# Attention loop of a fused perceiver layer: ScalarE spreads the turned output, GpSimd scales it by its reciprocals and adds the residual one batch later

## The reference, cut to what matters

```python
# x (16, 64, 1024); ctx (16, 1601, 256); mask (64, 1601)
q = layernorm(x).reshape(b, s, 8, 4, 32)                 # 8 kv heads, 4 query heads each
k = v = ctx.reshape(b, 1601, 8, 32)
scores = einsum('bsgrd,btgd->bgrst', q, k) / sqrt(32) + mask
out = einsum('bgrst,btgd->bsgrd', softmax(scores), v)
x = x + out.reshape(b, s, 1024)                          # this stage, the one that is changed
x = x + gated_ffn_with_top_k_zeroing(layernorm(x))       # untouched
x = x + mixture_of_8_low_rank_experts(layernorm(x))      # untouched
```

## Time and profile before

| | |
|---|---|
| median of 3 runs | 1584.75 us (1582.42 to 1586.70) |
| profiled execution, its own time | 1583.21 us |
| its span in the trace | 1580.8 us |
| attention loop, first to last mask addition | 45 to 645 us |
| PE, DVE, ACT, POOL busy, whole span | 1402, 1066, 664, 849 us |

### The profile page before, as it was taken

One profiled execution on the slowest core, in us unless ns is written; L12 is line 12 of the kernel. 1 busy time (PEld: TensorE's weight loads), 2 busy tenths in 40 slices (PEclk: granted clock), 3 DMA queues, 4 the chain that ended last, 5 costly groups with the idle time before them and its releaser, 6 DMA issues.

```text
span 1580.8 us, 30023 instructions
## 1 busy us (share of the span) xinstructions
PE 1402.1 (89%) x12775; PEld 1033.1 (65%) x12775; DVE 1065.7 (67%) x1424; ACT 664.1 (42%) x777; POOL 848.9 (54%) x410
## 2 busy tenths in 40 slices
PE   3899999999998999489999999999897788899975
PEld 3554555455554555289999998878776667687852
DVE  7788888888888888580000008998819888855663
ACT  2777777777777777312111116152410320011211
POOL 0577777777777777522233222333335565587840
PEclk9999999999999999789999999999999998899997
DMA  7032322232222230312322245565537855765612
GB/s 283 2 101 83 110 100 100 98 109 101 99 85 98 85 111 2 149 43 72 116 100 72 101 144 192 178 227 199 195 118 279 293 179 173 279 191 176 178 66 81
DMA packets 111466, 212.18 MB, mean 134 GB/s; under 512 B 8208, under 2 KB 84064, under 8 KB 107232
## 3 DMA queue, kind: packets, MB, share of 16 engines
q1 hardware_dynamic: 90224, 187.67, 34.6%
q10 hardware_dynamic: 21104, 22.55, 4.7%
HBM read 167.99 MB, written 42.21 MB: 133 GB/s over the span
## 4 chain that ended last, share of the span: by engine, by line
PE 42%; DVE 7%; DMA 4%; issue 3%; POOL 1%; ACT 1%; SPq 0%; DVEq 0%; ACTq 0%; POOLq 0%
PE ffn_bank L1794 15%; PE ffn_bank L1817 13%; PE ffn_bank L1848 11%; DMA ffn_u_raw<-w_up_t 2%; DVE ffn_h_lo L1497 1%; PE ffn_bank L1910 1%; PE ffn_bank L1875 1%; PE ffn_bank L1831 1%; DVE ffn_ln_stats L98 1%; DMA ffn_sx<-s 1%; DVE ffn_below L1393 1%; DMA sk<-ffn_sx 1%; DMA ffn_xt<-x 1%; POOL ffn_u_lo L1339 0%; DVE ffn_db L1408 0%
## 5 line engine op out<-in xcount | busy, mean ns | idle before, releaser
L761 POOL TENSOR_TENSOR fast_pair<-fast_probs 128x1024 f32<-128x1024 f32 x192 | 462.9, 2411 | 184.5 <-ACT fast_probs L879 107.4
L817 DVE TENSOR_TENSOR fast_masked<-fast_scores,fast_mask_t 128x1024 f32<-128x1024 f32 (+1 forms) x416 | 490.0, 1219 | 72.4 <-PE fast_scores L937 66.1
L879 ACT ACTIVATE fast_probs<-fast_masked 128x1024 f32<-128x1024 f32 (+1 forms) x416 | 440.0, 1058 | 145.4 <-DVE fast_masked L817 131.0
L937 PE MATMUL fast_scores<-fast_qT,fast_kraw 32*128 32x256 f32 (+1 forms) x3328 | 242.7, 406 | 46.7 <-DVE fast_masked L817 45.9
L937 PEld LDWEIGHTS fast_scores<-fast_qT,fast_kraw 32*128 32x128 f32 (+1 forms) x3328 | 150.4, 183 | 135.0 <-DVE fast_masked L817 94.7
L954 PE MATMUL fast_o_acc<-fast_probs,fast_vraw 128*32 128x256 f32 (+1 forms) x3328 | 228.4, 389 | 1.7 <-ACT fast_probs L879 1.7
L1794 PE MATMUL ffn_bank<-ffn_g_hi,ffn_z_hi 128*128 128x344 f32 x512 | 165.9, 324 | 2.6 <-ACT ffn_res L1658 2.6
L1382 DVE TENSOR_SCALAR ffn_cut<-ffn_total 128x2 f32<-128x2 f32 x4 | 0.7, 166 | 246.7 <-ACT ffn_mag L1662 246.7
L1351 POOL TENSOR_TENSOR ffn_d_lo<-ffn_d_raw,ffn_d_hi 128x1024 fp32r<-128x1024 f32 x66 | 163.2, 2472 | 5.3
L1794 PE MATMUL ffn_bank<-ffn_g_lo,ffn_z_hi 128*128 128x344 f32 x512 | 164.8, 322 | 0.0
L1794 PE MATMUL ffn_bank<-ffn_g_hi,ffn_z_lo 128*128 128x344 f32 x512 | 164.6, 322 | 0.0
(11 more groups left out here) (147 smaller groups left out, 1924.9 us busy)
## 6 DMA issues: line engine op xcount, KB each, us to landing
ffn_d_raw<-w_down SPq DMA_DIRECT2D x63, 512.0 KB, 3.7
fast_kraw<-ctx_t SPq DMA_DIRECT2D x32, 800.5 KB, 5.8
fast_vraw<-ctx_nat SPq DMA_DIRECT2D x16, 1536.0 KB
ffn_g_raw<-w_gate SPq DMA_DIRECT2D x8, 1376.0 KB
s<-ffn_res SPq DMA_DIRECT2D x8, 1376.0 KB, 6.1
ffn_mag<-s SPq DMA_DIRECT2D x8, 1376.0 KB, 9.8
ffn_sx<-s SPq DMA_DIRECT2D x8, 1376.0 KB, 6.9
sk<-ffn_sx SPq DMA_DIRECT2D x8, 1376.0 KB, 6.3
```

The lines of the kernel that those rows point to most:

```text
L761: pool.tensor_tensor(pair[:, n % PAIRS], both[:, :, 0, :], both[:, :, 1, :], ALU.add).then_inc(paired, 1)
L817: dve.tensor_tensor(into, of, m, ALU.add).then_inc(mask_added, 1)
L879: act.activation(probs[0:r, g % RING, hp * HALF:(hp + 1) * HALF], masked[0:r, h % SLOTS, :], ACT.Exp).then_inc(exp_done, 1)
L937: last = pe.matmul(scores[0:r, (2 * g + h // 2) % SLOTS, h % 2, i * 256:(i + 1) * 256], kraw[q, b % BUFS, u, c * P:c * P + r], qT[q, b, u, ...
```

## The change

ScalarE gets a new step, `spread_output` (L910 on in the changed file, its copies are L919), at the step of the turn, behind that step's exponentials. It copies the turned numerators from PSUM to `xo` in final order, two copies of 64x256, unscaled. VectorE's `normalise` keeps only two reciprocals of 64x8, written in the order of the heads, and now waits for both `o_turned` and `o_spread`; what it signals is `rden_ready`, for which TensorE's `weigh` waits in place of `o_normed`. Once a tile GpSimd multiplies all 128x1024 of `xo` by the reciprocals, broadcast over 32 elements each (`scale_output`, L764), in the `LAST` step after the tile's last normalisation, and adds `xres` (`add_residual`, L768) in the `LAST` step of the next batch. `xo` has two buffers. The store of a tile stands one batch later in SyncE's queue. For the last tile, the multiplication and the addition follow directly after the last reciprocals.

```diff
+        SPREAD1_AT = 17
+        SPREAD0_AT = 10
+        SCALE_AT = PER + 19
+        ADD_AT = SCALE_AT + PER
...
-                if b >= 3 and b % 2 == 1:
-                    sp.wait_ge(x_added, b // 2)
+                if b >= 4 and b % 2 == 0:
+                    sp.wait_ge(x_added, b // 2 - 1)
...
+            def scale_output(t):
+                pool.wait_ge(o_spread, 4 * t + 4)
+                pool.wait_ge(rden_ready, 4 * t + 4)
+                rows_of = xo[:, t % 2, :].rearrange("p (m d) -> p m d", d=HD)
+                by = rden[:, t].rearrange("p u g q h -> p (u g q h)").unsqueeze(2).broadcast_to([P, NH, HD])
+                pool.tensor_tensor(rows_of, rows_of, by, ALU.mult).then_inc(o_normed, 1)
+
+            def add_residual(t):
+                pool.wait_ge(o_normed, t + 1)
+                pool.tensor_tensor(xres[:, t, :], xo[:, t % 2, :], xres[:, t, :], ALU.add).then_inc(x_added, 1)
...
+            for g in range(GROUPS + 7):
+                if g < GROUPS:
+                    add_pair(g)
+                if g >= SCALE_AT and (g - SCALE_AT) % (2 * PER) == 0:
+                    scale_output((g - SCALE_AT) // (2 * PER))
+                if g >= ADD_AT and (g - ADD_AT) % (2 * PER) == 0:
+                    add_residual((g - ADD_AT) // (2 * PER))
+            add_residual(TILES - 1)
...
                 dve.wait_ge(o_turned, n + 1)
-                dve.reciprocal(rden[:, n], turned[:, 1, :, :, 0]).then_inc(rden_ready, 1)
-                dve.wait_ge(rden_ready, n + 1)
-                out = xo[b2 * S:(b2 + 1) * S, :].rearrange("s (u g q h d) -> s u h q g d", u=2, g=HALF_G, q=2, h=2)
+                dve.wait_ge(o_spread, n + 1)
+                out = rden[b2 * S:(b2 + 1) * S, t].rearrange("s u g q h -> s u h q g")
                 for h in range(2):
-                    half = slice(h * S, (h + 1) * S)
-                    last = dve.tensor_tensor(out[:, u, h], turned[half, 0],
-                                             rden[half, n].unsqueeze(3).broadcast_to([S, 2, HALF_G, HD]), ALU.mult)
-                last.then_inc(o_normed, 1)
-                if b2 == 1 and u == 1:
-                    dve.wait_ge(o_normed, n + 1)
-                    dve.tensor_tensor(xres[:, t, :], xo[:, :], xres[:, t, :], ALU.add).then_inc(x_added, 1)
+                    last = dve.reciprocal(out[:, u, h], turned[h * S:(h + 1) * S, :, :, 0])
+                last.then_inc(rden_ready, 1)
...
+            def spread_output(n):
+                b, u = divmod(n, 2)
+                t, b2 = divmod(b, 2)
+                act.wait_ge(o_turned, n + 1)
+                if b2 == 0 and u == 0 and t >= 2:
+                    act.wait_ge(x_added, t - 1)
+                out = xo[b2 * S:(b2 + 1) * S, t % 2, :].rearrange("s (u g q h d) -> s u h q g d", u=2, g=HALF_G, q=2, h=2)
+                for h in range(2):
+                    turned = o_acc[h * S:(h + 1) * S, u, 0:256].rearrange("p (q g d) -> p q g d", q=2, g=HALF_G)
+                    last = act.copy(out[:, u, h], turned)
+                last.then_inc(o_spread, 1)
...
-                        pe.wait_ge(o_normed, 2 * (b - 1) + u + 1)
+                        pe.wait_ge(rden_ready, 2 * (b - 1) + u + 1)
```

More of the change, by code:

```diff
@@ L661, in attention_fast @@
         od_sb = sb("od_sb", [P, 512], F32)
-        rden = sb("rden", [P, UNITS, 2, HALF_G], F32)
-        inside = sb("inside", [P, UNITS * 2 * HALF_G], F32)
+        rden = sb("rden", [P, TILES, 2, HALF_G, 2, 2], F32)
+        inside = sb("inside", [P, TILES * NH], F32)
         row_inside = sb("row_inside", [S, 1], F32)
-        xo = sb("xo", [P, D], F32)
+        xo = sb("xo", [P, 2, D], F32)
         eye = sb("eye", [P, P], F32)
@@ L692, in attention_fast @@
         rden_ready = sem("rden_ready")
+        o_spread = sem("o_spread")
         o_normed = sem("o_normed")
@@ L741, in _ @@
                     load_v(sp, b + BUFS)
-                if b >= 3 and b % 2 == 1:
-                    sp.wait_ge(x_added, b // 2)
-                    sp.dma_start(x1[(b // 2 - 1) * P:(b // 2) * P, :], xres[:, b // 2 - 1, :]).then_inc(x1_stored, 16)
-            sp.wait_ge(x_added, TILES)
-            sp.dma_start(x1[(TILES - 1) * P:TILES * P, :], xres[:, TILES - 1, :]).then_inc(x1_stored, 16)
+                if b >= 4 and b % 2 == 0:
+                    sp.wait_ge(x_added, b // 2 - 1)
+                    sp.dma_start(x1[(b // 2 - 2) * P:(b // 2 - 1) * P, :], xres[:, b // 2 - 2, :]).then_inc(x1_stored, 16)
+            for t in range(TILES - 2, TILES):
+                sp.wait_ge(x_added, t + 1)
+                sp.dma_start(x1[t * P:(t + 1) * P, :], xres[:, t, :]).then_inc(x1_stored, 16)
             sp.wait_ge(x1_stored, 16 * TILES)
@@ L752, in _, with add_pair @@
             pool.memset(ones[:, :], 1.0).then_inc(ones_ready, 1)
-            for g in range(GROUPS):
+            def scale_output(t):
[7 more added lines that the diff above has]
+                pool.tensor_tensor(xres[:, t, :], xo[:, t % 2, :], xres[:, t, :], ALU.add).then_inc(x_added, 1)
+            def add_pair(g):
                 if g % PER == LAST:
-                    continue
+                    return
                 n = pairs_before(g)
@@ L822, in normalise @@
                 t, b2 = divmod(b, 2)
[L823 removed]
+                turned = o_acc[:, u, 256:512].rearrange("p (q g d) -> p q g d", q=2, g=HALF_G)
                 dve.wait_ge(o_turned, n + 1)
[L825 to L827 removed]
+                dve.wait_ge(o_spread, n + 1)
+                out = rden[b2 * S:(b2 + 1) * S, t].rearrange("s u g q h -> s u h q g")
                 for h in range(2):
[L829 to L835 removed]
+                    last = dve.reciprocal(out[:, u, h], turned[h * S:(h + 1) * S, :, :, 0])
+                last.then_inc(rden_ready, 1)
             for g in range(GROUPS + 8):
@@ L843, in _ @@
                         normalise(2 * ((g - at) // PER) + u)
-            every = rden[:, :, :, :].rearrange("p n q g -> p (n q g)")
+            dve.wait_ge(rden_ready, UNITS)
+            every = rden[:, :, :, :, :, :].rearrange("p t u g q h -> p (t u g q h)")
             dve.tensor_scalar(inside[:, :], every, RDEN_LEAST, None, ALU.is_ge).then_inc(checked, 1)
@@ L888, in _ @@
             act.wait_ge(mask_turned, 1)
-            for g in range(GROUPS + 4):
+            def spread_output(n):
[9 more added lines that the diff above has]
+                last.then_inc(o_spread, 1)
+            for g in range(GROUPS + 6):
                 if g < GROUPS:
@@ L895, in _ @@
                         copy_output(2 * ((g - at) // PER) + u)
+                for u, at in ((0, SPREAD0_AT), (1, SPREAD1_AT)):
+                    if g >= at and (g - at) % PER == 0 and (g - at) // PER < B:
+                        spread_output(2 * ((g - at) // PER) + u)
         @block.tensor
```

1 line of the change is left out of this document (removed).

## The result

The changed kernel took 1543.66 us (median of 4 runs, 1540.49 to 1551.21) against 1583.59 of the kernel before beside it (4 runs, 1581.32 to 1586.70). The ratio is 0.9753, 95% interval 0.9713 to 0.9794. Repeated on other chips it took 1546.94 and 1549.67 us (5 runs each; ratios 0.9775, interval 0.9747 to 0.9804, and 0.9776, interval 0.9756 to 0.9796). The median of all 14 runs is 1546.7.

The account below looks back on a forecast made before the run. The ring between TensorE's scores and VectorE's mask additions was taken as the bound. Savings of 20.5 + 11.5 + 4.9 us less 3.8 at the stage's end gave 33.1 less: forecast 1551 us, range 1545 to 1563.

Parts of the forecast that it names:

- What bounds the kernel: Attention loop: TensorE's scores and VectorE's mask additions set the pace; VectorE delays beyond 0.15 us a step lengthen it.
- The multiplications: VectorE between mask additions: two multiplications go, two short reciprocals stay, saving 0.66 us in each of 31 halves, 20.5 us.
- The residual's addition: VectorE's L835 leaves the attention loop seven times at 1.64 us each, saving 11.5 us.
- TensorE's slow stretches: Clock falls after three of the loop's seven residual additions vanish, saving 1.63 us each, 4.9 us.
- ScalarE's copies: Two copies a half behind the turn's exponentials, 0.65 us together, fit ScalarE's idle gap and cost nothing in the loop.
- GpSimd: Its two new instructions a tile, 2.41 us each, fit idle time in LAST steps and cost nothing in the loop.
- The end of the stage: After the last turn, uncovered copies, reciprocals, multiplication and addition take 6.2 us until the store, 3.8 us more.
- The rest: Time outside the attention stage, taken as unchanged from the profiled execution of the kernel before.
- 1 (reciprocals of 0.43 us): VectorE's loop reciprocals cost as much as half-partition multiplications, saving 8 instead of 20.5 us: about 1564 us, chance 0.10.
- 2 (a slow broadcast): GpSimd's broadcast multiplication takes 7.2 us, three times an addition, partly uncovered: about 1569 us, chance 0.05.
- 3 (VectorE waits for `o_spread`): VectorE blocks on ScalarE's copies before mask additions, costing 38.4 us in the loop: about 1609 us, chance 0.04.
- 4 (GpSimd the bound): Nothing hides GpSimd's new instructions; fourteen in the loop cost 33.7 us: about 1584 us, no change, chance 0.02.

Follow-up runs that it names:

- the addition alone: Kernel before with only the residual's addition moved from VectorE to GpSimd and two buffers for xo: 1566.36 us, ratio 0.9893.
- the normalisation alone: Changed kernel with the residual's addition back on VectorE, two steps behind GpSimd's multiplication: 1557.02 us, ratio to the kernel before 0.9832.
- reciprocals twice: Changed kernel with both reciprocals of each half taken a second time into an unread buffer: 1562.67 us, ratio to the kernel before 0.9863.

## Why the forecast held in its mechanism and missed in its size

**What bounds the kernel: right.** The ring of scores and mask additions set the pace. Of work put between mask additions 0.39 to 0.42 of 0.43 us a half came out as time; work taken from there came back.

**The multiplications, 31 x 0.66 = 20.5 us: 1.6 us too high.** The mean gap between the mask additions around a half, without the residual's addition, went from 1.036 us to 0.428, so 0.61 a half and 18.9 in all. The length taken for a reciprocal, 0.20 us, was right (0.21). What was off is that all halves were taken to be alike: in the 15 of odd batches the reciprocals start 0.11 us later, and 15 x 0.12 = 1.8, of which the gap of before, 1.036 for 1.03, gives back 0.2.

**The residual's addition, 7 x 1.64 = 11.5 us: right.** Over the 31 halves the gaps sum to 43.65 us before and 13.26 now, 30.4 less: 18.9 and 11.5.

**TensorE's slow stretches, 4.9 us: right within what is left.** The loop is 34.8 us shorter, so 4.4 remain for them, and the addition alone, 16.2 us, gives 16.2 - 11.5 = 4.7. Both are remainders; the gaps between mask additions with nothing between them, which sum to 53.5 us before, to 49.4 in the changed kernel and to 48.5 with the addition alone, bear them out.

**ScalarE's copies: 0.74 us instead of 0.65, cost nothing in the loop, right.** The estimate by columns was low by 0.04 each.

**GpSimd: right, for nothing in the loop.** The multiplication is 1.92 us, not 2.41, and the room of 5.6 us that the forecast added up was measured at 5.6.

**The end of the stage, 3.8 us: 3.5.** The copies and hand-overs were a little longer, the multiplication shorter. GpSimd's two instructions lie over VectorE's check of the reciprocals, and L869 is held until L764 is over, 2.01 us instead of the 0.43 that it took before:

```profile
653.60 0.43 DVE L848 SCALAR_TENSOR_TENSOR fast_inside<-fast_rden,fast_inside 128x256 f32<-128x256 f32 x1
```

That costs nothing, as the store comes later still. The Trainium skill ("GPSIMD Engine Reference", § Key points) names a cause: GpSimd shares its SBUF interfaces with VectorE, and they contend where VectorE's instruction has two SBUF inputs or runs in a two-port mode. The trace agrees: L869 has two SBUF inputs and ends at 619.84, 0.28 us after L764. The forecast applied it to L835 and the mask additions and didn't look where else in the program the two engines meet.

**The sum: 33.1 us forecast, 31.3 measured in the stage** (30.9 as the mean of three profiles, 657.46 less 626.59). By itself the stage would have brought the time to about 1553.

**The rest, taken as fixed: this step failed and put the result outside the range.** The forecast carried over the 923.3 us of one profiled execution. It is 1.8 us above the mean of that kernel, 921.5, and the four runs of the changed kernel had 912.4 to 921.9, mean 916.0: 7.3 us less than carried over, against which stand the 1.8 too many in the stage. The other 2 us of the miss of 7.3 are the 0.9 by which 1551 stands above the sum's 1550.1, for the median of the runs, and the 1.1 by which the median of the four lies under their mean. The range was made of the bounds of the edits alone, though the spread of 4 us in the three runs of before showed that the untouched part moves as well. Over 14 runs the changed kernel's median is 1546.7 us, inside the range and 4 below the forecast, so a part of the miss is chance: the four runs of the result have the lowest mean rest of the three calls. Another part, the 3.7 us between the two kernels' mean rests, stays open.

**The rivals.** 1 (reciprocals of 0.43 us) fell: 0.21. 2 (a slow broadcast) fell: 1.92, shorter than an addition. 3 (VectorE waits for `o_spread`) fell: the copies end 1.27 us before. 4 (GpSimd the bound) fell, and two more additions a batch show where it would begin.

**A rival that the forecast hasn't, and no run tests.** The change does two things to the multiplications: it gives them to GpSimd, and it makes one instruction of 128x1024 a tile out of eight of 64x256. On VectorE those eight took 0.42 us each, 3.4 together; one of 128x1024 takes it 1.23 at the stage's end. Placed where VectorE waits 1.02 us for TensorE, like the addition of the normalisation alone, it might cost some 1.2 us a tile. By this estimate, 7 x 1.2, about 8 us of the 18.9 would be lost without GpSimd, and some 10 would come from the spreading and merging alone. Neither figure is shown.

## What to carry to other kernels

In a ring of engines with 0.15 us of slack a step, an instruction on the ring's engine is worth its length less the idle time at its place: 0.61 us out of the half's 1.04 between mask additions, and only 1.16 for an addition of 2.21 us that stood where the engine waited anyway. GpSimd, beside the ring, takes 1.95 and 2.40 us for what takes VectorE 1.23 each at the stage's end, and in the loop it costs nothing, as long as its room (gap plus time until its result is asked for, here 5.6 us a batch) isn't used up; so work out the room before the length. And a forecast of a whole time needs the scatter of the part that isn't touched, here 3 to 4 us of standard deviation, in its range.

## What the runs showed of the hardware

- A GpSimd multiplication of 128x1024 whose second input is broadcast over 32 elements takes 1.92 us, an addition of two full inputs 2.38.
- VectorE's instructions on SBUF can be held for the whole length of a GpSimd one: L110 takes 0.81 us, and 6.44 when it starts 0.21 us after a GpSimd instruction of 6.11. In each of the 28 places of the 13 traces where one of the stage's first five L110 meets a GpSimd cast or subtraction, it ends 0.55 us after that instruction; once it had started 0.08 us before it and was held all the same (6.70 us, "reciprocals twice"). Mask additions, with one input in PSUM, keep their 1.22 us beside GpSimd.
- A pair of short reciprocals starts 0.11 us later behind a mask addition when it writes partitions 64 to 127 than when it writes 0 to 63, in each of 15 and 16 halves; a second pair behind the first doesn't. No run here tells why.
- A reciprocal of 64x8 from PSUM takes 0.21 us and one of 128x32 from SBUF, eight times the elements, takes 0.34.
